# Handing the softmax maxima to the scores' operand: 8 rows per half chosen by half, or all 16 rows to both halves

## The reference

```python
# self-attention, x normalised over its features first
Q, K, V = (x @ W.T + b, split into 16 heads of 16)
scores = einsum('bhqd,bhkd->bhqk', Q, K) * scale
attn = softmax(scores, axis=-1)
x = x + einsum('bhqk,bhkd->bhqd', attn, V) @ Wo.T + bo
# cross-attention: the same with K, V from ctx, and masked keys set to a score of 1e-9
scores = where(mask == 0, 1e-9, scores)
# feed-forward
h = layernorm(gelu(x @ ternary(W_fc).T)); x = x + h @ ternary(W_proj).T
```

## Time and profile before

| | |
|---|---|
| median of three runs | 2536.92 us (2531.93 to 2538.22) |
| the profiled execution's own time | 2538.22 us |
| its span, first to last instruction | 2536.4 us |
| TensorE matmuls busy | 2205.3 us (87%) |
| VectorE busy | 2036.5 us (80%) |
| ScalarE busy | 1605.6 us (63%) |
| GpSimd busy | 1029.3 us (41%) |
| mean granted TensorE clock | 0.97 of full speed |
| moved by DMA | 268.62 MB |

### The profile page before, as it was taken

One profiled execution on the slowest core, in us unless ns is written; L12 is line 12 of the kernel. 1 busy time (PEld: TensorE's weight loads), 2 busy tenths in 40 slices (PEclk: granted clock), 3 DMA queues, 4 the chain that ended last, 5 costly groups with the idle time before them and its releaser, 6 DMA issues.

```text
span 2536.4 us, 70786 instructions
## 1 busy us (share of the span) xinstructions
PE 2205.3 (87%) x29031; PEld 1450.3 (57%) x29031; DVE 2036.5 (80%) x4025; ACT 1605.6 (63%) x2354; POOL 1029.3 (41%) x719
## 2 busy tenths in 40 slices
PE   3678898888889888889888888989865899999999
PEld 2435555555555555555555555555533677777776
DVE  7558888888888888888888888888753788888887
ACT  2346666666666666666666666666532777877876
POOL 2133433443344344434433443443221545555553
PEclk7789999999999999999999999999987999999999
DMA  6266676666677666666766666676431233233232
GB/s 138 44 114 110 121 128 117 121 115 121 115 124 125 117 115 119 121 116 123 121 123 115 119 120 119 119 123 117 78 62 45 75 92 99 77 96 94 79 100 59
DMA packets 441568, 268.62 MB, mean 106 GB/s; under 512 B 298320, under 2 KB 391888, under 8 KB 441296
## 3 DMA queue, kind: packets, MB, share of 16 engines
q1 hardware_dynamic: 438192, 264.37, 53.7%
q10 hardware_dynamic: 3104, 0.34, 0.1%
HBM read 54.87 MB, written 33.55 MB: 35 GB/s over the span
## 4 chain that ended last, share of the span: by engine, by line
SPq 35%; PE 35%; DVE 13%; DMA 8%; issue 6%; ACT 3%; POOL 1%; DVEq 0%; ACTq 0%; POOLq 0%
SPq L594 30%; PE ybk L1358 9%; PE hbk L1382 8%; PE product_bank L1027 5%; PE tbk L1372 4%; SPq L600 4%; DMA self_stk<-self_negmT 4%; DMA cross_stk<-cross_negmT 2%; DVE cross_mx L831 2%; DVE out_bank L863 2%; PE score_bank L949 2%; PE score_bank L969 2%; SPq L644 1%; PE exp_bank L987 1%; ACT prob L731 1%
## 5 line engine op out<-in xcount | busy, mean ns | idle before, releaser
L731 ACT ACTIVATE prob<-exp_bank 128x1024 f32<-128x1024 f32 x512 | 523.3, 1022 | 273.4 <-PE exp_bank L987 267.1
L831 DVE TENSOR_REDUCE cross_mx<-score_bank 128x8 f32<-128x1024 f32 x256 | 311.3, 1216 | 137.1 <-PE score_bank L969 136.8
L663 POOL TENSOR_TENSOR xs<-xn,xs 128x1024 f16<-128x1024 f32 x64 | 136.3, 2129 | 672.3 <-ACT xs L758 672.3
L831 DVE TENSOR_REDUCE self_mx<-score_bank 128x8 f32<-128x1024 f32 x256 | 310.5, 1213 | 98.9 <-PE score_bank L969 98.8
L663 POOL TENSOR_TENSOR ahl<-attT,ahl 128x512 f16<-128x512 f32 x128 | 148.2, 1158 | 349.9 <-ACT ahl L736 349.9
L1382 PE MATMUL hbk<-wfcT,ffn_xhl 128*128 128x512 f16 x1024 | 262.2, 379 | 6.4 <-ACT hid L1279 3.6
L1342 DVE SCALAR_TENSOR_TENSOR ghl<-tbk,lnwc,ghl 128x512 f16<-128x512 f32 x256 | 188.0, 735 | 98.1 <-ACT ghl L1273 98.0
L1358 PE MATMUL ybk<-wpT,ghl 128*128 128x256 f16 x2048 | 260.4, 273 | 0.8 <-DVE ffn_y L1327 0.7
L1358 PEld LDWEIGHTS ybk<-wpT,ghl 128*128 128x128 f16 x2048 | 197.9, 98 | 66.1 <-DVE ghl L1342 0.9
L1273 ACT ACTIVATE ghl<-tbk,lnwc 128x512 f16<-128x512 f32 x256 | 174.3, 682 | 67.5 <-PE tbk L1372 67.5
L863 DVE STREAM_TRANSPOSE out_bank<-out_bank 128x512 f32<-128x512 f32 x256 | 184.0, 719 | 37.5 <-PE out_bank L1004 37.4
(11 more groups left out here) (159 smaller groups left out, 4653.6 us busy)
## 6 DMA issues: line engine op xcount, KB each, us to landing
self_stk<-self_qk SPq DMA_DIRECT2D x768, 64.0 KB, 2.4
cross_stk<-cross_qk SPq DMA_DIRECT2D x768, 64.0 KB, 2.4
self_src<-in_x SPq DMA_DIRECT2D x32, 512.0 KB, 4.8
ctx_in<-in_ctx SPq DMA_DIRECT2D x32, 512.0 KB, 5.6
x_scratch<-xn SPq DMA_DIRECT2D x32, 512.0 KB, 4.3
ffn_src<-x_scratch SPq DMA_DIRECT2D x32, 512.0 KB, 3.8
out<-ffn_y SPq DMA_DIRECT2D x32, 512.0 KB, 3.6
self_stk<-self_negmT SPq DMA_DIRECT2D x64, 64.0 KB
```

The costliest lines, as they stand in the source:

```text
L663: nc.gpsimd.tensor_tensor(out, src, hi, ALU.subtract).then_inc(lo_ready, 1)
L731: act.activation(prob[:, p % 3], ebank[:, :, :], ACT.Exp, scale=EXP_SCALE).then_inc(b.exp_done, 1)
L831: dve.tensor_reduce(a.mx[:, g * H:(g + 1) * H].rearrange("p (r e j) -> p r e j", r=2, e=2)[:, :, eight], sbank[:, :, :].rearrange("p r (j ...
```

## The change

The maxima's rows in each half become 16 instead of 8. Before, the DMA of half r carries rows 8r to 8r + 7 of `negmT`, for which VectorE writes the maxima in an order that puts the heads of a half next to each other. After, both DMAs carry all 16 rows, the heads stand in their natural order, and `sel` picks row 2j + 8k + r. The second pass's matmuls contract over 64 rows of a half and not 56. The instructions of each engine stay the same in number, kind and order; what differs is the shape of the two DMAs of a slot (8 x 8 x 512 elements before, 16 x 8 x 512 after), the depth of the contraction, the order in which VectorE writes 8 maxima, and the strides with which TensorE reads `negm` in the cross chain.

```diff
-SHIFTED = STACK + FT
...
 # setup, the table of the chosen row
                 nc.gpsimd.affine_select(out=sh.sel[:, :, :], in_=sh.sel[:, :, :], compare_op=ALU.not_equal, fill=SHIFT,
-                                        base=-(HALF * r + STACK), pattern=[[-1, FT // 2], [-FT // 2, KT]],
+                                        base=-(HALF * r + STACK + r), pattern=[[-2, FT // 2], [-FT, KT]],
...
 # sp_slot, maxima
                     for r in range(2):
-                        sp.dma_start(a.stk[HALF * r + STACK:HALF * r + SHIFTED, s.ra, 0].rearrange("p j k t -> p (j k) t"),
-                                     a.negmT[FT * r:FT * (r + 1), :].unsqueeze(1).broadcast_to([FT, FT, T])).then_inc(a.m_in, 16)
+                        sp.dma_start(a.stk[HALF * r + STACK:HALF * (r + 1), s.ra, 0].rearrange("p j k t -> p (j k) t"),
+                                     a.negmT[:, :].unsqueeze(1).broadcast_to([H, FT // 2 * KT, T])).then_inc(a.m_in, 16)
...
 # dve_slot, maximum
-                    g, eight = divmod(m, 2)
-
-                    dve.tensor_reduce(a.mx[:, g * H:(g + 1) * H].rearrange("p (r e j) -> p r e j", r=2, e=2)[:, :, eight],
+                    dve.tensor_reduce(a.mx[:, 8 * m:8 * m + 8].rearrange("p (j r) -> p r j", r=2),
                                       sbank[:, :, :].rearrange("p r (j k) -> p r j k", j=4), AX.X, ALU.max).then_inc(a.max_done, 1)
...
 # pe_slot, shifted
-                        rows = slice(HALF * r, HALF * r + SHIFTED)
+                        rows = slice(HALF * r, HALF * (r + 1))
...
 # pe_slot, turn_maxima, cross chain alone
-                                             a.negm[:, :].rearrange("p (b r q c) -> p r c b q", r=2, q=QUADS, c=2)[:, jq % 2, jq // 2], start=True, stop=True, skip_group_check=True)
+                                             a.negm[:, :].rearrange("p (a j) -> p j a", j=4)[:, jq], start=True, stop=True, skip_group_check=True)
```

## The result

The changed kernel takes 2553.93 us (median of 6 runs, 2548.52 to 2555.81) against 2535.06 us before (6 runs, 2526.55 to 2539.03). The ratio is 1.0072, 95% interval 1.0052 to 1.0090: slower by 18.9 us. The forecast was 2529 us, and the range to 2548 does not hold the time. It went the way of rival C, though not for the reason that C gave first: the rate nearly doubled.

The account below looks back on a forecast made before the run. Hand-overs bound the kernel, each slot's cycle closing through the maxima's landing. Savings of 0.21 us per self and 0.1 per cross slot made 10 us; four fifths, 8 us, took 2538.22 to 2530.2, median 2529 us; range 2508 to 2548.

Parts of the forecast that it names:

- rival C: Both maxima DMAs: 16 rows don't double the rate, landing later; 2569 us at 80 GB/s, 2708 at 49; chance 0.17.
- The chain and its closing through the landing: Each slot's cycle closes through the landing of the maxima wherever TensorE waits for it; idle 23.5 us in 37 waits.
- The cap of 0.64 us in each of 64 slots: TensorE's waits for the maxima: an earlier landing gains at most about 0.64 us a slot, 41 us over 64.
- Matmuls and VectorE at 0: 64-row contraction, strided read of negm and VectorE's order of maxima: taken to cost 0.
- The issue at 600 ns: Maxima DMA issues on SyncE's queue fall from 720 to 600 ns, worth 0.1 us a slot.
- The transfer at twice the rate: Maxima DMAs on 16 rows: rate doubles from 49 to 98 GB/s, 256 KB take 2.67 us, nothing gained or lost.
- 1.85 + 2.67: Maxima landing before: 1.85 us fixed plus 2.67 for two transfers gives 4.52 from first issue, against 4.53 in the chain.
- What runs beside the second maxima DMA: The load behind the maxima queues behind them instead of running beside: 0.11 us less in self slots, 0 in cross.

Follow-up runs that it names:

- e1: Kernel before with only its two maxima DMAs changed to the 16-row form, contraction still over 56 rows: 2548.95 us, ratio 1.0088.
- e15: Changed kernel with negmT copied out twice by ScalarE, both maxima DMAs still reading the first copy: 2557.66 us, ratio 1.0096.
- e2: Changed kernel with the maxima DMAs back at 8 rows from the third group of a chain on, the rest as changed: 2533.71 us, ratio 1.0012.
- e6: Kernel before with both 8-row maxima DMAs reading rows 0 to 7 of negmT: 2569.66 us, ratio 1.0153.
- e7: Changed kernel with the load issued ahead of the store in cross slots, no wait added: 2543.08 us, ratio 1.0048.
- e12: Changed kernel with negmT kept twice, at partitions 0 to 15 and 64 to 79, the odd half's DMA reading the second copy: 2544.36 us, ratio 1.0058.
- e13: Changed kernel with negmT kept twice, the odd half's DMA reading the second copy, and the load ahead of the store in cross slots: 2531.31 us, ratio 0.9994.
- e14: Kernel before with the load issued ahead of the store in cross slots: 2537.33 us, ratio 1.0020.
- e3: Changed kernel with SyncE's queue waiting in cross slots until the maxima have landed before issuing store and load: 2540.85 us, ratio 1.0050.
- e4: Kernel before with SyncE's queue waiting in cross slots until the maxima have landed before issuing store and load: 2538.55 us, ratio 1.0029.
- e8: Changed kernel with each of the 16 rows sent to 4 of its 8 places from the third group on: 2516.23 us, ratio 0.9936.

## Why the prediction was wrong

**The chain and its closing through the landing: right in the mechanism, rough in the size.** The idle time of matmuls for the maxima grew by 17.9 us and the time by 18.9. Over the kernels of the table, 32 slots times the two landings' difference to before gives 28 us for after (18.9 measured), 28 for e1 (18) and e15 (26), -1 for e2 (3), 37 for e6 (36), 11 for e7 (10), 18 for e12 (13), -6 for e13 (-0.5) and 8 for e14 (5.5); with the added wait, 7 for e3 (10) and -1 for e4 (8). The waits for the maxima alone don't carry it: e7 has 22.7 us of them, no more than before, and is 10 us slower. The cap of 0.64 us in each of 64 slots, 41 us, was read too high from the rows: they have 23.5 us in 37 slots, and e8 came out 17 below before.

**Matmuls and VectorE at 0: right** within what can be told (e2: 3 us, 0 to 6). **The issue at 600 ns: right**, 598.

**The transfer at twice the rate: nearly right in the rate, wrong in the comparison.** "256 KB take 2.67 us: nothing gained, nothing lost." The windows show 89 and 93 GB/s, so 2.82 to 2.95 us. That is the smaller part. The 49 GB/s came from stretches that hold the first DMA alone, and "two take 2.67" gave it to both; e4 shows the second one at 109 GB/s and the pair done in some 2.2 us. That 1.85 + 2.67 met the measured 4.53 us was luck, and it hid this. e6 shows that the second DMA of the kernel before profits from reading rows 8 to 15 and not rows 0 to 7 again, by about 0.5 us in self slots. The change takes that away. The second copy (e12) gives 0.27 us back. I had named it, "both DMAs now read the same 16 rows", in support of rival C, and priced it at nothing in the sum.

**What runs beside the second maxima DMA: wrong in sign, and the largest error.** The step read "with all 16 engines taken by the maxima, the load queues behind them", took 0.11 us back in self slots and 0 in cross slots. In self slots the load's 0.2 us stayed (e3's landing without a follower in cross slots is 3.82 after the second issue, with a load 3.99). In cross slots the store costs 0.68 us where it had cost nothing: cross landing 5.13 us and not 4.23, the table's 4.33 less the forecast 0.1. Of the 0.80 us by which it grew, 0.64 are the store's (0.68 less 0.04) and 0.16 the pair's own. As self and cross differed before by 0.22 us with a load or a store behind, I took the store for harmless. It is, as e4 shows, while the maxima are 8 rows at a share of about one half. That the store must share all engines and reads SBUF as the maxima do is a possible reason that no run tests; what e3, e4, e7 and e14 show is the delay, not how it is made.

**Rival C** had the right side and place, but decided by a rate that fails to double ("It turns slower from about 92 GB/s on"). The measured 89 and 93 lie at that point and explain little of the loss; 2569 us at 80 GB/s is above the time. Its 0.15 of a slower result was too little, since a doubling of bytes ahead of the wait that closes the cycle had two ways to go wrong and was priced at one.

## What to carry to other kernels

Before widening a transfer that a chain waits for, look at what stands behind it on the queue and in which direction that moves: here a store behind it turned from harmless to 0.68 us. Where two DMAs run in a row, read the rate of each by itself; here the second one was twice as fast as long as it read other rows than the first, and a source that both read in full took that away. More rows per DMA save nothing unless bytes per row fall too: here twice the rows cost 19 us, and half of the copies on the same 16 rows took the time from 2553.93 to 2516.23 us.

## What the runs showed of the hardware

A DMA from 8 rows to 8 took 720 ns to issue and ran at a DMA share near one half; from 16 rows to 16, 598 ns and 0.83 to 0.92. The first 8-row DMA of a pair moved 46 to 53 GB/s, the second one, from other rows, 109 (e4); pairs that both read the same 16 rows kept 89 to 102 throughout (after, e3). Two 8-row DMAs that read the same rows landed 0.5 to 0.7 us later than two that read different ones (e6). A 512 KB store issued right behind 16-row DMAs, with a load behind it, delayed their landing by 0.68 us, a load of the same size in first place by 0.2 (e3, e7); behind 8-row DMAs the store delayed nothing that counts, 0.04 us (e4).
